# A decoder layer on one core: row maxima in halves over ScalarE's DMA queue, second pass eight slots behind the first, cross queries through DRAM

## The reference, cut to what matters

```python
# x, ctx: (4, 256, 128); 16 heads of 8; softmax over 256 keys
x = x + self_attn(layernorm(x))         # rotary on q and k, causal mask, out @ Wo.T
x = x + cross_attn(layernorm(x), ctx)   # q from x, k and v from ctx, @ W_proj + b_proj
x = x + moe(layernorm(x))               # 8 experts of 128 -> 512 -> 128, exact gelu
# moe: one routing per sequence: softmax(mean over tokens @ gate_w), top 2, weights normed
```

## Time and profile before

| | |
|---|---|
| median of 3 runs | 200.0 us (199.74 to 201.43) |
| profiled execution, its own time | 200.95 us |
| its span, first to last instruction | 199.2 us |
| mean granted TensorE clock | 0.947 of full |
| busy: TensorE, VectorE, ScalarE, GpSimd | 166.8, 140.7, 104.8, 52.3 us |
| TensorE idle for stackQ<-maxT (at L893) | 3.8 us in 6 waits |

### The profile page before, as it was taken

The page is one execution under the profiler, slowest core; times in us unless marked ns, Lnnn a source line. Parts: engine busy times, 40 slices in busy tenths (PEclk is TensorE's granted clock), DMA queues, the critical chain, the costliest instruction groups (busy, mean ns, idle before and its releaser), DMA issues.

```text
span 199.2 us, 4411 instructions
## 1 busy us (share of the span) xinstructions
PE 166.8 (84%) x1500; PEld 116.1 (58%) x1508; DVE 140.7 (71%) x545; ACT 104.8 (53%) x222; POOL 52.3 (26%) x103
## 2 busy tenths in 40 slices
PE   0686195699599979989998998998998899799994
PEld 0343184485466755755764655654665556598984
DVE  2789299897347899799799889888968346525020
ACT  2132021257147656566566666766676657793451
POOL 7810005668800070030030030010115107126050
PEclk9999669589769999999999999999999999999999
DMA  5817660058227503322321321300340350170720
GB/s 150 238 35 175 164 173 18 3 148 184 70 82 196 184 25 104 110 69 58 109 82 49 98 95 35 90 0 3 113 130 3 100 143 0 17 224 26 229 66 26
DMA packets 23842, 19.05 MB, mean 96 GB/s; under 512 B 2364, under 2 KB 21820, under 8 KB 23100
## 3 DMA queue, kind: packets, MB, share of 16 engines
q1 hardware_dynamic: 22908, 17.79, 31.9%
q10 hardware_dynamic: 912, 0.98, 2.0%
HBM read 12.54 MB, written 2.49 MB: 75 GB/s over the span
## 4 chain that ended last, share of the span: by engine, by line
PE 50%; DVE 19%; DMA 15%; SPq 5%; issue 4%; POOL 3%; ACT 2%; POOLq 0%; DVEq 0%; ACTq 0%
PE psV L914 11%; PE psB L893 9%; PE psA L868 8%; DMA stackQ<-maxT 6%; DMA stackQ<-scratch 4%; DVE masked L623 4%; PE psA L958 4%; PE psM L923 3%; PE psA L975 3%; DMA stackK<-hid 3%; PE psV L975 3%; PE psM L933 3%; DVE stats L554 2%; DVE negmax L629 2%; SPq L402 2%
## 5 line engine op out<-in xcount | busy, mean ns | idle before, releaser
L753 ACT ACTIVATE E<-psB 128x512 f32<-128x512 f32 x112 | 62.3, 595 | 37.3 <-PE psB L893 15.7
L868 PE MATMUL psA<-stackK,stackQ 72*128 72x256 bf16 (+1 forms) x256 | 44.4, 277 | 11.8 <-DMA stackK<-hid 5.5
L893 PE MATMUL psB<-stackQ,stackK 74*128 74x256 bf16 (+1 forms) x256 | 42.2, 264 | 4.6 <-DMA stackQ<-maxT 3.8
L623 DVE CUSTOM_DVE_ANT_0 masked<-psA,row_mask 128x128 bf16<-128x128 f32 (+1 forms) x128 | 36.8, 352 | 11.8 <-PE psA L868 11.7
L629 DVE TENSOR_REDUCE negmax<-psA 128x2 f32<-128x512 f32 x64 | 39.7, 677 | 0.0
L868 PEld LDWEIGHTS psA<-stackK,stackQ 72*128 72x128 bf16 x256 | 23.0, 105 | 21.5 <-DMA stackQ<-scratch 8.6
L914 PE MATMUL psV<-E,V 128*9 128x256 f32 (+1 forms) x512 | 30.9, 359 | 0.2 <-ACT E L753 0.2
L893 PEld LDWEIGHTS psB<-stackQ,stackK 74*128 74x128 bf16 x256 | 22.0, 100 | 12.5 <-DMA stackQ<-maxT 5.6
L468 POOL TENSOR_SCALAR rstd<-mv 128x2 f32<-128x2 f32 x12 | 2.8, 236 | 89.1 <-DVE mv L558 88.9
L914 PEld LDWEIGHTS psV<-E,V 128*9 128x9 f32 x512 | 11.0, 90 | 14.4 <-issue 7.9
L761 ACT ACTIVATE oT<-psV 128x256 f32<-128x256 f32 x32 | 12.3, 384 | 7.9 <-PE psV L914 7.2
(11 more groups left out here) (111 smaller groups left out, 247.0 us busy)
## 6 DMA issues: line engine op xcount, KB each, us to landing
stackK<-scratch SPq DMA_DIRECT2D x18, 192.0 KB
stackQ<-hid SPq DMA_DIRECT2D x36, 64.0 KB
w1s<-w_dram SPq DMA_DIRECT2D x8, 258.0 KB, 2.8
w2s<-w_dram SPq DMA_DIRECT2D x8, 256.0 KB, 3.7
stackQ<-scratch SPq DMA_DIRECT2D x3, 576.0 KB
stackK<-hid SPq DMA_DIRECT2D x18, 64.0 KB
scratch<-hid SPq DMA_DIRECT2D x4, 192.0 KB, 3.7
scratch<-parts_ctx SPq DMA_DIRECT2D x4, 192.0 KB, 4.7
```

Source lines behind the costliest of these rows:

```text
L623: last = dve.tensor_tensor_reduce(out=masked[:, bank, i * keys:(i + 1) * keys], in0=scores[:, i, 0:keys], in1=row_mask[:, S - keys:S], sca ...
L753: act.activation(dst, psB[:, bank].rearrange("p (h q) -> p h q", h=dst.shape[1]), ACT.Exp, scale=SCALE).then_inc(b_taken, 1)
L868: last = pe.matmul(psA[:, bank, i * keys:(i + 1) * keys], stackQ[0:ROWS, b, h, t * P:(t + 1) * P], stackK[0:ROWS, b, h, 0:keys], start=Tru ...
L893: last = pe.matmul(psB[:, bank, i * n:(i + 1) * n], stackK[:, b, h, t * P:(t + 1) * P], stackQ[:, b, h, q0:S], start=(s == 1 or i == 0), s ...
```

## The change

The distance between the passes, LAG, goes from eleven slots to eight. The row maxima are turned and sent in halves of eight heads: the old step becomes three. "max_turn" is the transpose on TensorE, "max_rows" VectorE's split, "row_out" the two transfers, issued by ScalarE and no longer by SyncE, with a semaphore for each half. For job 0 the three stand together at slots 4 and 8. For the others they stand at slots 8j + 4 and 8j + 8, with VectorE's part ahead of the slot's first units and the other two behind them. Cross queries are written to DRAM five slots behind o_turn ("stack_put") and read back two slots later ("stack_get"). The DRAM steps of sequences 2 and 3 are split into keys and queries and stand earlier. The projections of sequence 3 go to psV in place of a psB bank, so VectorE's initial memset of psV goes; the mask buffer has two slots in place of three. stack_read_k stays at slot 8b + 21. The first four moe_up move from -11..-8 to -8..-5 relative to `last`; in slot numbers the first four stay at 64 to 67, and the next four, before at 71 to 74, are at 68 to 71.

```diff
-FFN_STEPS = ((-11, "u0"), (-10, "u1"), (-9, "u2"), (-8, "u3"), (-4, "u4"), (-3, "u5"), (-2, "u6"), (-1, "u7"),
+FFN_STEPS = ((-8, "u0"), (-7, "u1"), (-6, "u2"), (-5, "u3"), (-4, "u4"), (-3, "u5"), (-2, "u6"), (-1, "u7"),
-LAG = 11
+LAG = 8
-    put(7, "max_rows", 0, 0)
-    put(9, "stack_write", 0, 2)
-    put(10, "stack_read", 0, 2)
-    put(14, "stack_write", 0, 3)
+    put(6, "stack_write", 0, 2, 1)
+    put(9, "stack_write", 0, 2, 0)
+    put(9, "stack_read", 0, 2, 1)
+    put(10, "stack_read", 0, 2, 0)
+    put(13, "stack_write", 0, 3, 1)
+    put(14, "stack_write", 0, 3, 0)
+    put(14, "stack_read", 0, 3, 1)
+    put(15, "stack_read", 0, 3, 0)
...
-        if j > 0:
-            put(n + 2 * NG, "max_rows", s, b)
-        if j == 1:
-            put(n + 2 * NG + 1, "stack_read", 0, 3)
+        for half in range(2):
+            if j == 0:
+                put(NG * (half + 1), "max_turn", 0, 0, half)
+                put(NG * (half + 1), "max_rows", 0, 0, half)
+                put(NG * (half + 1), "row_out", 0, 0, half)
+            else:
+                row_of[n + NG * (half + 1)] = (s, b, half)
...
-            put(m, "stack_read_k", 1, b)
+            put(n + 21, "stack_read_k", 1, b)
             put(m + 5, "q_cross", 1, b)
-            put(m + 5, "stack_fill", 1, b)
+            put(m + 5, "stack_put", 1, b)
+            put(m + 7, "stack_get", 1, b)
...
+        if half in row_of:
+            order.append(("max_rows", *row_of[half]))
         order += [step for _, step in sorted(units, key=lambda unit: unit[0])]
+        if half in row_of:
+            order += [("max_turn", *row_of[half]), ("row_out", *row_of[half])]
...
-        masked = sb("masked", [P, NA, 2 * S], BF16)
+        masked = sb("masked", [P, 2, 2 * S], BF16)
-        maxT = sb("maxT", [NT * NH, NB, 2, P], BF16)
+        maxT = sb("maxT", [NT * NH // 2, NB, 2, 2, P], BF16)
+        def qk_bank(b):
+            return psB[:, b % 2] if b < 3 else psV
...
+                if kind == "stack_put" and s == 1:
+                    sp.wait_ge(parts_q[b], NPART)
+                    write_parts(s, b, 0, parts[:, b, 0], scr_q[b])
+                if kind == "stack_get" and s == 1:
+                    sp.wait_ge(scr_q[b], 16)
+                    read_q(s, b)
...
+                if kind == "row_out":
+                    bank, k = row_use[s, b, g]
+                    act.wait_ge(misc_taken[bank], k)
+                    heads = slice(g * NH // 2, (g + 1) * NH // 2)
+                    for i in range(2):
+                        act.dma_start(stackQ[MAXROW + i:MAXROW + i + 1, b, heads].rearrange("o h (t q) -> o (h t) q", t=NT),
+                                      maxT[:, b, g, i, :]).then_inc(maxrow_in[g][b], 16)
...
-                if kind == "max_rows":
-                    pe.wait_ge(a_taken, a_units_until(job))
-                    pe.transpose(psM[0:NT * NH, bank, 0:P], negmax[:, b], ident[:, :]).then_inc(misc_full[bank], 1)
+                if kind == "max_turn":
+                    pe.wait_ge(a_taken, a_units_until(job * NG + 2 * g + 1))
+                    heads = slice(g * NH // 2, (g + 1) * NH // 2)
+                    pe.transpose(psM[0:NT * NH // 2, bank, 0:P], negmax[:, b, heads],
+                                 ident[:, :]).then_inc(misc_full[bank], 1)
                 if kind == "scores_exp":
                     u, bank = st["u"], unit % 2
-                    if g == 0 and u == 0:
-                        pe.wait_ge(maxrow_in[b], 32 * (s + 1))
+                    if g % 2 == 0 and u == 0:
+                        pe.wait_ge(maxrow_in[g // 2][b], 32 * (s + 1))
```

More of the change, by code:

```diff
@@ L161, in plan @@
     uses = {"ln_turn": 1, "v_self": 1, "ctx_turn": 1, "k_cross": 1, "v_cross": 1, "q_cross": 1,
-            "max_rows": 1, "o_turn": 2, "o_back": 1, "o_proj": 1, "route": 1}
+            "max_turn": 1, "o_turn": 2, "o_back": 1, "o_proj": 1, "route": 1}
     count, total, steps = [0, 0], 0, []
@@ L183, in plan, with a_units_until @@
     return steps, a_unit, b_unit
-def a_units_until(job):
-    return sum(NG * GRP_UNITS[j // NB] for j in range(job + 1))
+def a_units_until(group):
+    return sum(GRP_UNITS[n // (NG * NB)] for n in range(group + 1))
 def b_units_until(group):
@@ L199, in build @@
     use = {(st["kind"], st["s"], st["b"]): st["misc"] for st in steps if st["misc"]}
+    row_use = {(st["s"], st["b"], st["g"]): st["misc"][0] for st in steps if st["kind"] == "max_turn"}
     scratch = nc.dram_tensor("scratch", [2, NB, 2, NPART, P, S], BF16).ap()
@@ L398, in _ @@
                     read_k(s, b)
-                if kind == "max_rows":
-                    sp.wait_ge(misc_taken[st["misc"][0][0]], st["misc"][0][1])
-                    for i in range(2):
-                        sp.dma_start(stackQ[MAXROW + i:MAXROW + i + 1, b].rearrange("o h (t q) -> o (h t) q", t=NT),
-                                     maxT[:, b, i, :]).then_inc(maxrow_in[b], 16)
                 if kind == "route_pick":
@@ L544, in rope_terms @@
                                   ALU.mult).then_inc(sem_done, 1)
-            dve.memset(psV[:, :], 0.0).then_inc(v_zeroed, 1)
             for st in steps:
@@ L571, in _ @@
                         dve.wait_ge(parts_q_self[b - 2], NPART)
[L572 removed]
+                    rope_terms(qk_bank(b), rot[:, b % 2], rope_first)
                     if b < 2:
@@ L619, in _ @@
                             dve.wait_ge(row_mask_set, 1)
-                        if unit >= NA:
-                            dve.wait_ge(a_taken, unit - NA + 1)
+                        if unit >= 2:
+                            dve.wait_ge(a_taken, unit - 1)
                         for i in range(nh):
-                            last = dve.tensor_tensor_reduce(out=masked[:, bank, i * keys:(i + 1) * keys], in0=scores[:, i, 0:keys],
+                            last = dve.tensor_tensor_reduce(out=masked[:, unit % 2, i * keys:(i + 1) * keys], in0=scores[:, i, 0:keys],
                                                             in1=row_mask[:, S - keys:S], scale=-1.0, scalar=LARGEST,
@@ L816, in _ @@
                     taken("ln_turn", 0, b)
-                    if b >= 2:
-                        pe.wait_ge(rope_first, b - 1)
+                    if b == 2:
+                        pe.wait_ge(rope_first, 1)
                     for w in range(2):
-                        last = pe.matmul(psB[:, b % 2, w * S:(w + 1) * S], wQK[:, w, :], xnT[:, b, :], start=True,
+                        last = pe.matmul(qk_bank(b)[:, w * S:(w + 1) * S], wQK[:, w, :], xnT[:, b, :], start=True,
                                          stop=True)
@@ L890, in _ @@
                     if unit < 2:
-                        pe.wait_ge(rope_first, unit + 3)
+                        pe.wait_ge(rope_first, 3 - unit)
                     for i, h in enumerate(heads):
```

62 lines of the change are left out of this document (28 added, 34 removed).

## The result

The changed kernel takes 211.94 us (median of 4 runs, 210.41 to 213.41), the kernel before 200.13 us (4 runs). The ratio is 1.058 with an interval of 1.051 to 1.064: slower by 11.8 us, where 3.2 us less was forecast. The profiled execution of after has a span of 210.4 us at a mean granted clock of 0.926, against 199.2 us at 0.947. Some executions of every kernel here run in a slower state, at a lower granted clock; the ratios leave them out and the medians do not, so that a ratio can differ from that of two medians.

A forecast was written before the change was run, and what follows sets the result against it. VectorE's instruction stream, not the row transfer, was taken to pace the middle stage. Terms - 2.5 + 2.4 + 1.8 - 4.9 = - 3.2 us gave 196.8 us from the 200.0 median; own range 195 to 198.5, eight-in-ten range 193.0 to 201.5.

The forecast's parts named there:

- Step (1): Head, slots 8 to 17: second pass starts at slot 8, not 11; gain 2.5 us, bounds 0 and 5.
- rival (d): Job 1's second pass waits for late row transfers sharing engines with 576 KB reads; 199.3 us; chance 0.25 with (a).
- (a): Head: the fill gains nothing, TensorE idles before slot 16, then half clock; 199.3 us, no change; chance 0.25 with rival (d).
- Step (4): ScalarE's queue: issuing 32 row transfers takes 3.6 us a job from ScalarE, which stays below the period; cost 0.
- Rival (b): Row steps, twice a job: ScalarE becomes the bound if an issue exceeds about 1.08 us; + 6.3, 203.1 us; chance 0.10.
- Steps (2) and (3): Slots 18 to 63: row maxima by halves, net + 2.4 us; then work pulled ahead, + 1.8 us on VectorE.
- Chain view (c): Middle: seven row transfers bound the jobs, VectorE's new pauses lie in wasted time, + 3.5 falls away; 193.3 us; chance 0.15.
- step (3): Slots 60 to 63: at distance eight job 5's output step falls within them, not behind; + 1.8 us on VectorE.
- Step (5): Cross queries through DRAM, one write and one read a job replacing nine copies; cost 0, bounds 0 and + 1.
- Step (6): End, last first-pass unit to last "values": second-pass work and waits gone from this stretch; - 4.9 us.

The follow-up runs named there:

- the twin: The mended kernel with the 32 row transfers issued by ScalarE again instead of SyncE; 203.87 us, 1.017 (1.010 to 1.024).
- the mended kernel: Changed kernel with rows issued by SyncE, job 0's upper row step ahead of rope(0, 3), job 3's stack reads at slot 16; 199.05 us, 0.995; repeated 199.09 us, 0.998.

## Why the prediction was wrong, step by step

**Step (1), the head, is the one that failed.** It forecast a gain of 2.5 us with bounds of 0 and 5, and slot 18 at 56.1; it was at 66.6, 7.9 us later than before. That is 10.4 of the 14.4 us between the forecast of the span and what came. I had added TensorE's work to the time in which it was already busy and called the rest cover. The step missed two things. First, the order within slot 8: I listed what the change puts into slots 8 to 17 by kind and not in the order in which each engine meets it. Row_out stands behind rope(0, 3), ScalarE stands still there for 3.63 us, and kc, v_self and the next first-pass unit stand behind ScalarE. Moved, it gives 8 us of the span back (210.4 to 202.1 us; the ratio falls from 1.058 to 1.009). Second, the transfers: I wrote "nothing waits for them" of the queries, and priced the rows' own transfer at 1.86 us, from a stretch without stack reads; beside them it took 7.52 us, and TensorE stood for 3.18. That was rival (d), whose mechanism was right and whose price, "it is (a) in time", was far too low. The two are not independent: with rope moved the lower rows go out ahead of the reads.

The cover itself held. With both stalls gone, slots 8 to 12 are 4.5 us longer than before, but slot 18 comes at 57.6 (57.5 repeated), 1.1 us earlier than before: inside the bounds, and less than half of the 2.5 us. The sum for TensorE (+ 2.4 us up to 51.9) used durations at full clock, and slots 8 to 12 ran at 0.71. How much of the shortfall that is, is not shown: the twin at full clock was only 0.8 us earlier at slot 16, but with ScalarE's waits.

**Step (4), "Cost 0", failed too**, on a smaller scale, and it is also what gave step (1) its stall. An issue costs what I said (median 594 ns against SyncE's 589); the lock rule of the Trainium skill, Perfetto Trace Analysis, section "DMA Instruction — HWDGE (DVE, Sync)", decided nothing: of 32 issues one took 1.42 us and one 1.03, both where SyncE issued nothing, and the one that met an issue of SyncE (52.81) took 0.87. The standstill in the middle was priced right as well: I took 1.8 us a step, and the waits before oT are 15.1 us in 8, 1.9 us each, of which 1.15 are the two issues (in slot 8 it was 3.63). What was wrong is the inference from "it stays below the period" to "Cost 0". TensorE's waits for the exponentials, from slot 24 to 63, in the kernel before, in after and in the mended kernel:

```profile
PEld psB L893 <- ACT E L753: 1.3, 6, 0.3
...
PEld psB L913 <- ACT E L771: 5.5, 13, 1.2
...
PEld psB L915 <- ACT E L773: 1.4, 5, 0.3
```

VectorE's waits for the transpose are the same 3.5 us in 6 in the last two, so they do not make the difference. With ScalarE's rows the middle takes 77.7 to 79.6 us (after, and the runs with rope moved), with SyncE's 76.0 to 76.1 in four profiles of three kernels; in time it is 2%. Rival (b) had the place right and named the wrong quantity: not an issue of more than 1.08 us, but what is queued behind the wait. ScalarE is busy 47.64 of 79.6 us there, so it is not full; the group's next product needs oT out of the one psV bank. The Trainium skill, DMA: Bandwidth & Descriptors, section "Issuing engines are not separate DMA queues", says that starting transfers on several engines saves only sequencer time. The runs do not contradict it (an issue is 0.59 us on either engine), and add a cost: where the issuing engine computes, what is queued behind its wait for the source is late too, 20 us in all with the rows of the kernel before.

**Steps (2) and (3), slots 18 to 63,** had + 4.2 us together. The waits at o_proj went, as written. The waits for the transpose came ten times, as written; from slot 18 on they are 4.7 us in 7 (0.67 each, forecast 0.5) in after. The sum came to + 9.0 us in after, with ScalarE's waits in it, and to + 5.3 us in the mended kernel (91.5 against 86.2 us). It does not lie where I put it. The period of a job hardly grows: slots 24 to 56, four jobs, take 63.0 us in the mended kernel and 62.5 before, 0.1 us a job in place of the 0.4 that the period of 16.1 implied. Chain view (c) has some truth then; part of the pauses lies in time in which VectorE would have waited anyhow. And 4.5 of the 5.3 us come in slots 18 to 24, where job 0's output step is pulled ahead: that is the mechanism of step (3), which I had counted for job 5 alone. How the + 5.3 us divide between the two steps was not measured.

**Step (5)** was right: 0.995, with 1 inside the interval. **Step (6)** was right: forecast 4.9 us less and 20.7 us from the end of the first pass, measured 6.0 and 19.9, with the 28.6 us behind it unchanged. It is the largest gain that the runs show, and each slot of distance is worth some 1.9 us of it.

Of the signs that I named beforehand, the one of (a), "a gap of TensorE before job 2's first unit, with half clock behind it", came nearly so: the gap before 60.38 has half clock behind it, but stands behind that unit (56.81), and what ends it is the rows of (d) and not the queries of (a). The price was wrong: rival (a) priced the stall at the loss of the 2.5 us gained, and the two stalls made slot 18 7.9 us later than before.

**A better version.** The mended kernel is 6% faster than the changed one and, by 0.995 (0.990 to 1.000) and 0.998 (0.993 to 1.003), equal to the kernel before or half a per cent ahead. Its spans are 197.7 and 197.2 us against 199.2, a gain of 1.5 to 2.0 where the sum had 3.2: 1.1 up to slot 18, 5.3 (4.9) lost from there to slot 63, and 5.7 won behind it. Open are how much less slots 18 to 24 could take, and the odd distances.

## What to carry to other kernels

When a transfer's issue is moved to an engine that computes, walk that engine's program from the wait on: price the time until the source is ready, not the issue alone, and name what the next instruction feeds; then put whatever delays the source (here rope, 2 us of VectorE) behind it. Small transfers that something waits for soon have to be priced beside the largest transfer that can be in flight at that slot, not from a quiet stretch. A sum of busy times gives only the floor of a stretch in which the engines hand work to each other through one or two banks.

## What was not expected of the hardware

A transfer of 4 KB landed in 1.6 us at best and in 8.2 us at worst in after. The four slowest (5.3 to 8.2 us) were issued within 1 us of the issue of a stack read of 192 or 576 KB; it happened from ScalarE's queue (7.52 us) as from SyncE's (6.64, in the run with the rows on SyncE). TensorE's granted clock was 0.50 from 37 to 49 us in after, though it worked without a gap from 37 to 41 and from 45 to 49; in the kernel with the rows ahead of rope it was 0.65 from 41 to 45 and 1.00 from 45 to 49. Two kernels that differ only in the queue of the rows had 1.00 and 0.54 in the same four microseconds of the head, and two profiles of the mended kernel had 0.61 and 0.77 from 41 to 45 us, so the clock of one stretch should not be put down to an edit from one profile.
